# Transposing the adjacency matrix with 32x32 VectorE blocks and a block-exchanging load in place of TensorE, in an eight-graph GNN kernel

## The reference

```python
H = (adj != 0)                                  # [C, C]
w = adj[0, :]                                   # first row of adj
conv(x, W, b) = Dn * (H @ (Be * (H.T @ (x @ W.T)))) + b
    # Dn = 1 / (H @ w) per node,  Be = 1 / column sums of H
h = layer_norm(relu(conv(x, W1, b1)), gamma, beta)
x1 = layer_norm(x + (conv(h, W2, b2) + x))
agg = (adj @ x1) / max(row sums of adj, 1e-6)
out = layer_norm(x1 + relu(concat(x1, agg) @ WL.T))
```

## Time and profile before

| | |
|---|---|
| Time, median of 3 runs (lowest to highest) | 1166.24 us (1166.12 to 1166.53) |
| Span of the profiled execution | 1165.3 us |
| What the median has beside that span | 0.9 us |
| PE, busy in matmuls | 1143.4 us (98%) |
| DVE, busy | 688.6 us (59%) |
| ACT, busy | 370.2 us (32%) |
| POOL, busy | 143.2 us (12%) |
| Mean granted clock of TensorE | 0.996 |

### The profile page before, as it was taken

The page is one execution under the profiler, slowest core; times in us unless marked ns, Lnnn a source line. Parts: engine busy times, 40 slices in busy tenths (PEclk is TensorE's granted clock), DMA queues, the critical chain, the costliest instruction groups (busy, mean ns, idle before and its releaser), DMA issues.

```text
span 1165.3 us, 18227 instructions
## 1 busy us (share of the span) xinstructions
PE 1143.4 (98%) x6560; PEld 948.4 (81%) x6560; DVE 688.6 (59%) x1783; ACT 370.2 (32%) x816; POOL 143.2 (12%) x95
## 2 busy tenths in 40 slices
PE   6799999999999999999999999999999999999998
PEld 6669798696987969779797887968789697896976
DVE  5663468634686447755478463783647735587335
ACT  4243313422234222342233331433314333044230
POOL 1102002120111102011020110201102011020100
PEclk9899999999999999999999999999999999999999
DMA  7103010130110301112001210013000130000001
GB/s 266 55 1 145 1 37 1 54 144 0 36 40 14 144 0 36 54 40 103 9 27 54 99 45 18 18 54 144 0 18 18 54 144 0 27 10 0 1 1 36
DMA packets 29316, 56.77 MB, mean 49 GB/s; under 512 B 2416, under 2 KB 19440, under 8 KB 29296
## 3 DMA queue, kind: packets, MB, share of 16 engines
q1 hardware_dynamic: 29296, 56.50, 13.5%
HBM read 48.11 MB, written 8.39 MB: 48 GB/s over the span
## 4 chain that ended last, share of the span: by engine, by line
PE 97%; DVE 1%; issue 1%; DMA 1%; SPq 0%; ACT 0%; DVEq 0%; ACTq 0%
PE bank L662 40%; PE bank L724 10%; PE bank L687 10%; PE bank L762 9%; PE bank L784 9%; PE bank L746 9%; PE bank L696 4%; PE bank L754 2%; PE bank L770 1%; DMA W1n<-in_L_gnn_W_dram 1%; DVE H L440 0%; PE bank L647 0%; DVE unread L448 0%; DVE HT L487 0%; PE bank L651 0%
## 5 line engine op out<-in xcount | busy, mean ns | idle before, releaser
L662 PE MATMUL bank<-yv,adjT 128*128 128x257 f32 x1024 | 223.3, 379 | 0.0
L662 PEld LDWEIGHTS bank<-yv,adjT 128*128 128x128 f32 x1024 | 193.6, 189 | 31.8 <-issue 3.8
L358 ACT ACTIVATE small<-mv,small 128x1 f32<-128x1 f32 x192 | 56.5, 295 | 352.1 <-DVE mv L475 256.5
L687 PE MATMUL bank<-x_hi,H 128*128 128x258 f32 x512 | 134.7, 296 | 7.3 <-DVE H L440 6.7
L480 DVE SCALAR_TENSOR_TENSOR m_lo<-bank,small,m_hi 128x256 fp32r<-128x256 f32 x128 | 61.0, 482 | 120.7 <-ACT m_hi L353 120.7
L662 PE MATMUL bank<-x_hi,H 128*128 128x256 f32 x512 | 122.6, 283 | 0.0
L662 PE MATMUL bank<-m_hi,HT 128*128 128x256 f32 x512 | 121.5, 280 | 0.0
L662 PE MATMUL bank<-x_lo,H 128*128 128x256 f32 x512 | 121.1, 280 | 0.0
L662 PE MATMUL bank<-m_lo,HT 128*128 128x256 f32 x512 | 120.8, 279 | 0.0
L746 PE MATMUL bank<-W1T,zT 128*128 128x512 f32 x256 | 120.3, 592 | 0.0
L762 PE MATMUL bank<-gW2T,xnT 128*128 128x256 f32 x512 | 119.8, 379 | 0.0
(11 more groups left out here) (75 smaller groups left out, 1676.2 us busy)
## 6 DMA issues: line engine op xcount, KB each, us to landing
raw<-in_adj_dram SPq DMA_DIRECT2D x32, 1024.0 KB, 8.9
x_in<-in_x_dram SPq DMA_DIRECT2D x8, 1024.0 KB, 6.7
out_dram<-xres SPq DMA_DIRECT2D x32, 256.0 KB, 2.1
w_row<-in_adj_dram SPq DMA_DIRECT2D x8, 512.0 KB, 3.9
W2n<-in_L_gnn_W_dram SPq DMA_DIRECT2D x1, 512.0 KB, 3.7
W1n<-in_L_gnn_W_dram SPq DMA_DIRECT2D x1, 512.0 KB, 7.8
WLn<-in_L_gnn_W_dram SPq DMA_DIRECT2D x1, 512.0 KB, 8.6
b_row<-in_L_gnn_b_dram SPq DMA_DIRECT2D x1, 256.0 KB, 15.5
```

The costliest lines, as they stand in the source:

```text
L358: nc.scalar.activation(std[:, i:i + 1], mv[:, which, i, 1:2], ACT.Sqrt, bias=eps_c)\
L662: last = mm(bank(stage, i)[:, 0:n_cols], lhsT, rhs, start=(k == 0 and part == 0), stop=(k == NT - 1 and part == parts - 1))
L687: last = mm(*args, start=(c == 0 and n == 0), stop=(c == NT - 1 and n == 1))
```

## The change

Graph 0 keeps the TensorE transposes. For graphs 1 to 7, `adjT` is built in two steps. First, 32 more DMAs per graph read adj a second time from DRAM and put its 32x32 blocks in exchanged places into `adjB`, which lies over `raw`. Then 8 VectorE instructions (`transpose_blocks`), one after each tile of L, transpose all 32x32 blocks of a tile. To make the blocks fit, node n now lies on partition n // 8, tile n % 8; so `raw`, `x_in` and `out` are loaded and stored in 8 KB or 2 KB pieces per partition, and a weight block of H is every eighth column (`H_columns`). The sums for Dn and `build_rDn` move ahead of L, since `adjB` overwrites `raw`. `HT` is written by row tiles (`build_HT_rows`), after the last transpose, and S2 waits for them one by one.

```diff
+    Q = 32
+    NB = P // Q
+    RB = C // NB
@@ load_graph, load_x, store
-                                 adj[b, 2 * j * P:(2 * j + 2) * P, :].rearrange("(t p) e -> p t e", p=P))\
+                                 adj[b, :, :].rearrange("(p t) e -> p t e", t=NT)[:, 2 * j:2 * j + 2, :])\
+            def load_adjB(b, t):
+                rows = adj[b, :, :].rearrange("(k r t) e -> t r k e", k=NB, t=NT)
+                for a in range(NB):
+                    sp.dma_start(adjB[a * Q:(a + 1) * Q, t, :, :], rows[t, :, :, a * RB:(a + 1) * RB])\
+                      .then_inc(adjB_loaded[t], 16)
@@ sync engine, one graph
                     load_graph(b + 1)
+                    for t in range(NT):
+                        sp.wait_ge(H_ready, (b + 1) * NT + t + 1)
+                        sp.wait_ge(dn_ready, (b + 1) * NT + t + 1)
+                        load_adjB(b + 1, t)
@@ scalar engine, S1 of the next graph
                     for e in range(NT):
-                        take_adjT(e, b + 1)
                         take_m_hi("S1", e, b + 1, e)
@@ vector engine
+            def transpose_blocks(t, b):
+                dve.wait_ge(adjB_loaded[t], (b - 1) * (16 * NB) + 16 * NB)
+                nc.vector.transpose(adjT[:, :, t * P:(t + 1) * P],
+                                    adjB[:, t, :, :].rearrange("p k (c j) -> p j k c", c=Q)).then_inc(adjT_ready, 1)
+            def build_HT_rows(k, b):
+                dve.wait_ge(adjT_ready, (b - 1) * NT + NT)
+                nc.vector.tensor_scalar(HT[:, k, :], adjT[:, k, :], 0.0, None, ALU.not_equal).then_inc(HT_ready, 1)
@@
                 if more:
+                    dve.wait_ge(q_split, b * NT + NT)
                     for c in range(NT):
                         build_H_tile(c, b + 1)
+                        sum_Dn(c, b + 1)
+                    build_rDn(b + 1)
@@ end of a tile of L
                         moments("o", 2, xres[:, i, :], i, b)
+                        if more:
+                            transpose_blocks(i, b + 1)
                 if more:
                     for e in range(NT):
-                        take_rBe(e, b + 1)
-                        if e > 0:
-                            build_HT(e - 1, b + 1)
-                        take_m_lo("S1", e, b + 1, e)
-                    build_HT(NT - 1, b + 1)
-                    for c in range(NT):
-                        sum_Dn(c, b + 1)
-                    build_rDn(b + 1)
+                        build_HT_rows(e, b + 1)
+                        if e >= 1:
+                            take_rBe(e - 1, b + 1)
+                            take_m_lo("S1", e - 1, b + 1, e - 1)
+                    take_rBe(NT - 1, b + 1)
+                    take_m_lo("S1", NT - 1, b + 1, NT - 1)
@@ tensor engine
+            def H_columns(c, e):
+                return H[:, c, :].rearrange("p (n t) -> p t n", t=NT)[:, e, :]
             def s1_step(e, c, b):
-                lhsT = H[:, c, e * P:(e + 1) * P]
+                lhsT = H_columns(c, e)
@@
-                pe.wait_ge(HT_ready, b * NT + NT // NCH)
                 for k in range(NT):
+                    pe.wait_ge(HT_ready, b * NT + max(NT // NCH, k + 1))
                     pe.wait_ge(*emptied("S1", k, b))
                     s2_step(0, k)
@@
-                      lambda c, e, part: (H[:, c, e * P:(e + 1) * P], (x_hi, x_lo)[part][:, c, 0:D]))
+                      lambda c, e, part: (H_columns(c, e), (x_hi, x_lo)[part][:, c, 0:D]))
@@
                             s1_step(e, c, b + 1)
-                        transpose_adj(e, b + 1)
```

More of the change, by code:

```diff
@@ L67, in graph_net @@
     assert NCH == 2 and NT == 8 and ND == 2 and NH == 4
+    Q = 32
+    NB = P // Q
+    RB = C // NB
+    assert RB == Q * NT
     DP = D + 2
     YP = 2 * D + 1
-    setup_fills = [1, 0, 0, 0, 0, 0, 3, 3]
-    setup_empties = [1, 1, 1, 1, 1, 1, 3, 3]
+    W_FILLS = 3
+    setup_fills = [1, 0, 0, 0, 0, 0, W_FILLS + NT, W_FILLS + NT]
+    setup_empties = [1, 1, 1, 1, 1, 1, W_FILLS + NT, W_FILLS + NT]
     bank_of, nth = {}, {}
@@ L90, in graph_net @@
         add_job("S1", e)
-        add_job("TA", 2 * e)
-        add_job("TA", 2 * e + 1)
     for j in range(NCH * ND):
@@ L152, in graph_net @@
         xnT, _, _ = place("xnT", [P, 2, NH, P], F32, nxt)
+        adjB, _, _ = place("adjB", [P, NT, NB, RB], F32, raw_at)
         yv, _, _ = place("yv", [P, NT, YP], F32, HT_at)
@@ L182, in graph_net @@
         raw_loaded = [sem(f"raw_loaded{n}") for n in range(NT // 2)]
+        adjB_loaded = [sem(f"adjB_loaded{n}") for n in range(NT)]
+        adjT_ready = sem("adjT_ready")
         x_loaded, w_loaded, W2_loaded, W1_loaded, WL_loaded, rows_loaded, bias_loaded, table_loaded = (
@@ L359, in root, with take_adjT @@
                   .then_inc(std_done[norm], 1)
-            def take_adjT(c, b):
+            def take_adjT(c):
                 for half in range(2):
[L364 to L368, removed]
+                    tb = TRANSPOSE_BANKS[half]
+                    act.wait_ge(bank_full[tb], W_FILLS + c + 1)
+                    nc.scalar.activation(adjT[:, half * 4:half * 4 + 4, c * P:(c + 1) * P],
+                                         banks[tb][:, :].rearrange("p (k c) -> p k c", c=P), ACT.Copy)\
+                      .then_inc(bank_empty[tb], 1)
             for c in range(NT - 1):
-                take_adjT(c, 0)
+                take_adjT(c)
             take_m_hi("S1", 0, 0, 0)
             take_m_hi("S1", 1, 0, 1)
-            take_adjT(NT - 1, 0)
+            take_adjT(NT - 1)
             for e in range(2, NT):
@@ L482, in take_m_lo, with build_HT_columns @@
                     in1=m_hi[:, e, :].bitcast(F32), op0=ALU.mult, op1=ALU.subtract), stage, e)
-            def build_HT(c, b):
-                dve.wait_ge(*emptied("TA", 2 * c, b))
-                dve.wait_ge(*emptied("TA", 2 * c + 1, b))
+            def build_HT_columns(c):
+                for tb in TRANSPOSE_BANKS:
+                    dve.wait_ge(bank_empty[tb], W_FILLS + c + 1)
                 nc.vector.tensor_scalar(HT[:, :, c * P:(c + 1) * P], adjT[:, :, c * P:(c + 1) * P], 0.0, None,
                                         ALU.not_equal).then_inc(HT_ready, 1)
+            def transpose_blocks(t, b):
[5 more added lines that the diff above has]
+                nc.vector.tensor_scalar(HT[:, k, :], adjT[:, k, :], 0.0, None, ALU.not_equal).then_inc(HT_ready, 1)
             for n in range(1, TRANSPOSE_BANKS[0]):
@@ L522, in _ @@
                 if c >= 2:
-                    build_HT(c - 2, 0)
-            build_HT(NT - 2, 0)
+                    build_HT_columns(c - 2)
+            build_HT_columns(NT - 2)
             n_side = TRANSPOSE_BANKS[0]
@@ L528, in _ @@
                 if e == 2:
-                    build_HT(NT - 1, 0)
+                    build_HT_columns(NT - 1)
                 if e + 1 < n_side:
@@ L689, in s1_step, with transpose_adj @@
                     fills_bank(last, "S1", e)
-            def transpose_adj(c, b):
-                for job in (2 * c, 2 * c + 1):
-                    pe.wait_ge(*free("TA", job, b))
+            def transpose_adj(c):
+                for half, tb in enumerate(TRANSPOSE_BANKS):
+                    pe.wait_ge(bank_empty[tb], W_FILLS + c)
                     for k in range(4):
-                        kt = job % 2 * 4 + k
-                        last = nc.tensor.transpose(bank("TA", job)[:, k * P:(k + 1) * P],
-                                                   raw[:, c, kt * P:(kt + 1) * P], ident[:, :])
-                    fills_bank(last, "TA", job)
+                        cols = raw[:, c, :].rearrange("p (n t) -> p t n", t=NT)[:, half * 4 + k, :]
+                        last = nc.tensor.transpose(banks[tb][:, k * P:(k + 1) * P], cols, ident[:, :])
+                    last.then_inc(bank_full[tb], 1)
             n_side = TRANSPOSE_BANKS[0]
@@ L709, in _ @@
                     s1_step(e, c, 0)
-                transpose_adj(c, 0)
+                transpose_adj(c)
             for e in range(n_side, NT):
```

7 lines of the change are left out of this document (4 added, 3 removed).

## The result

The changed kernel takes 1361.07 us (median of 4 runs, 1360.85 to 1362.03), the kernel before 1166.38 us beside it: a ratio of 1.167, 95% interval 1.165 to 1.169. It is slower by 195 us, where the forecast was 1166.5 us and the range ended at 1335. The profiled execution spans 1360.2 us. Two runs in the slower state, one of experiment 10 (2925.54 us) and one of the kernel before beside it (1194.22 us), are left out of the ratios.

A forecast was written before the change was run, and what follows sets the result against it. PE was taken to bound the kernel: 1165.3 us less 49 for removed transposes, plus 49 of waits for DVE and 0.9 beside the span, gave 1166.2, rounded up to 1166.5 us; range 1150 to 1335 us.

The forecast's parts named there:

- the part on the weights: Loads of `H` in S1 and S3 at a 32-byte step: taken as no change, at low confidence; upper bound twice 107 to 110 ns.
- The row: Profile row of a write: eight elements 2052 bytes apart take 65 ns against 59 ns for one; used for the weights' pace.
- The rule of the Trainium skill: SBUF lines are 16 bytes; two hits on a line are needed to hide latency, so a 32-byte step is slower.
- Weights at half pace: Rival for S1 and S3: each load of `H` takes 107 ns more, 1332 us in all; chance 0.28.
- The transposes: VectorE block transposes, one after each tile of L: 1.27 us each, from bounds of 0.60 and 2.5 us.
- within 10 us of that: With DVE's reads slow as well as the weights, the time stays within 10 us of the slow-weights rival's 1332 us.
- What is removed: TensorE transposes in S1, eight of 0.11 us per tile: 7.0 us per passage between graphs, 49 us over seven.
- DVE's list and POOL: DVE's work up to `m_lo` of tile 7, with two `HT` rows waiting out POOL instructions, turns the 7.0 us saved into waiting.
- the sum: DVE's list added up from 288.75: `m_lo` 7 done at 338.8, when PE reaches step 7 of S2's first chunk.
- The clock rival: PE's waits in S2 lower its clock to the 1.2 GHz level: 3 us more per passage, 1187 us; chance 0.07.
- The transfers: Second load of adj, 4 MB per graph: 16 us to issue, at most 22 us to move, landed by 295, costing nothing.
- What would show it: Trace signs: S1 rows of 1.91 us (3.6 if weights slow), S3 with S4 28.28, PE waits and full clock in S2.

The follow-up runs named there:

- experiment 10: Kernel of experiment 6 with POOL's first residual also held back and `raw` loaded tile by tile over 128 partitions: 1164.39 us, ratio 0.997.
- experiment 1: Kernel before, with only the weight blocks of `H` read at a step of 32 bytes in S1 and S3: 1410.64 us in one run.
- experiment 7: Changed kernel with weights read in order and `H` written by VectorE at a step of 512 bytes: 1206.8 us, ratio 1.031.
- experiment 6: Changed kernel re-laid so all reads have 128-byte runs, all graphs using block transposes, POOL's residual waiting for eight `HT` rows: 1136.16 us, ratio 0.973.
- Experiment 3: Changed kernel with the weights of `H` and the VectorE transposes both reading neighbouring elements: 1151.41 us, ratio 0.986.

## Why the prediction was wrong, and where it was right

**The step that failed** is the one in the part on the weights: "It is nearer to no change, and I take that". It put the price of TensorE's read at a step of 32 bytes at nothing, from a DVE write of eight elements. The runs showed 122 ns more for each load of `H`, 241 in place of 119, and experiment 1 shows it with nothing else changed: 243 us.

The row never spoke for no change. Its (65 - 59) / 7 = 0.9 ns is for each element more, and a load reads 128 elements from each partition; 128 x 0.9 = 110 ns, by this estimate, is the size of what was measured. The row also has no write of eight neighbouring elements beside it, so it can't tell the price of a step from the price of an element, and its 59 ns are of a write to a PSUM bank. Nor is a stepped access free on VectorE itself: a tile of `H` written at a step of 512 bytes takes 1.35 us in place of 0.75 (experiment 7), a transpose read at 32 bytes 2.07 us in place of 1.22. The rule of the Trainium skill quoted against the forecast held for the loads of `H` and for the block transposes. For the loads of `raw` in graph 0 it held for the load, 198 in place of 142 ns, and hardly for the distance. What spoke loudest was in the text and was not weighed: no slack at 110 to 119 ns, 2048 loads in S1 and S3, almost all of them on PE's path, so that each 10 ns is 20 us.

**The rival's size.** "Weights at half pace" had the mechanism and gave 1332 us, since it added 107 ns to a load. It had the chance 0.28, under the forecast's 0.32. The runs show 122 ns: S3 + 15.7 (forecast 13.7), a passage's S1 + 8.55 (forecast 6.6), graph 0 + 8.8 (forecast 10). 7 x 3.9 + 2.0 - 1.2 = 28 us, and 1332 + 28 = 1360. The bound was set too low: it took twice the pace as the worst case, and it doubled the 107 to 110 ns of the transposes instead of the 119 ns of S1 and S3. That put the measured time outside the range, which ended at 1335 us.

**The transposes.** Forecast 1.27 us from the distance of two sums. In order they have a distance of 1.07 us (tile of L 3.26 us instead of 3.46), stepped 2.03 to 2.07 us. With the weights slow as well they add nothing, as the rival said ("within 10 us of that").

**What is removed** was right: 49 us forecast, 48 us between experiment 1 and the changed kernel, and 134.58 us per passage in experiment 6.

**DVE's list and POOL** were right in the main, which could be seen only once the weights were read in order: PE waited in S2 for DVE, and DVE for POOL, and one wait moved took 4.9 us off each passage (experiment 6). Experiment 3 differs from the sum in three places. The transposes are 8 x 0.20 = 1.6 us shorter. `HT` row 2 starts at 315.16, 0.4 us ahead of POOL, so that rows 3 and 4 were held and not 2 and 3; the text named this ("saves about 1 us"). Together they bring the `m_lo` some 3 us sooner. And the wait that counts is another one: the sum holds PE at step 7 of S2 for `m_lo` 7, but PE was held at step 0, by `m_lo` 3 and its PSUM bank, a wait that the sum doesn't have. By the sum's own times it would have stayed hidden: `m_lo` 3 done at 331.8 and step 7, 26 matmuls later, at 337.9, before the 338.8 of `m_lo` 7. So a passage takes 139.5 us in place of 141.6, and the kernel 1151 in place of 1166 us.

**The clock rival** is in it as well: the fall to 0.57 is there, behind a stretch in which PE was busy for 1.13 of 4 us. It costs 1.8 us per passage, where the rival had 3. The forecast's sum for this case came near 1151 us in part by luck, since the clock that it left out and the list that it made too long pull in opposite ways.

**The transfers** were right: 4 MB in 16.6 us of issue at some 230 GB/s, bounded in the text by half of 386 GB/s.

**What would show it.** S1 was read off at 30.82 / 8 = 3.85 us a tile, the row named for slow weights; S3 with S4 at 43.95; no wait of DVE on `adjB`. The waits of PE in S2 and the clock of S2 could not be read in the changed kernel, since S1 covered them.

## What to carry to other kernels

An access pattern is a cost of the instruction that reads it, and must be priced on the engine that reads it, per load and times the number of loads on the path; when no row shows the pattern, a rule about it weighs more than a distant row of another engine, and the upper bound has to lie beyond twice the pace (here 241 on 119 ns). When a reordering makes one engine's data fit, look for a layout in which every reader meets neighbouring elements (here runs of 32, which with POOL's residual moved turned 1361 into 1136 us). Then look for the next thing that the removed time runs into: 5 of the 7 us per passage hung on two POOL instructions that could wait, and 1.8 of the 5 were the clock that fell behind the pause. List every wait of the engine on the path, those for a free PSUM bank too.

## What the runs showed of the hardware that was not expected

- Weight loads of 128x128 blocks of `H` (float32r) under matmuls of 256 columns: distance of matmuls 118 to 119 ns in order, 3 ns more at a step of 8 bytes, 235 at 16, 241 at 32; the load itself 189, 197, 328 to 331 and 338 ns.
- Weight loads of 128x128 blocks of `raw` (float32) for TensorE transposes, at a step of 32 bytes: the load 198 in place of 142 ns, the distance 114 in place of 109 ns.
- A VectorE transpose of 32x32 blocks, 1024 float32 per partition: 1.22 us from runs of 128 bytes, 2.03 to 2.07 us from elements 32 bytes apart. A one-source pass written with a step of 512 bytes: 1.35 us on the mean, in place of 0.75.
- A VectorE pass of 0.68 us that begins under a POOL instruction ends 0.56 us after it. Behind a pause of PE of 3.2 us the granted clock fell to 0.57 on the mean of 4 us, which cost 1.8 us.
- DMAs that cover 32 partitions move some 230 GB/s with all engines busy, those over 128 partitions mostly 406 to 437 GB/s, and those over 128 partitions whose outermost dimension is four 104 GB/s with a quarter of the engines.
